# Row sort on one core: the key minimum of the other lot stands between the two masked copies of a lot

## What is computed

```python
q1, k1, q2, k2, v = jnp.split(qkv, 5, axis=1)
vf = v.reshape(b, c, hw)
idx = jnp.argsort(vf, axis=-1)
vs = jnp.take_along_axis(vf, idx, axis=-1)
gat = lambda t: jnp.take_along_axis(t.reshape(b, c, hw), idx, axis=-1)
out1 = _reshape_attn(gat(q1), gat(k1), vs, temperature, True)
out2 = _reshape_attn(gat(q2), gat(k2), vs, temperature, False)
inv = jnp.argsort(idx, axis=-1)
out1 = jnp.take_along_axis(out1, inv, axis=-1)
out2 = jnp.take_along_axis(out2, inv, axis=-1)
```

## Time and profile before

| what | value |
|---|---|
| median of three runs (lowest, highest) | 14898.59 us (14898.33, 14907.5) |
| span of the profiled execution | 14884.8 us |
| DVE busy | 13771.3 us, 93% |
| ACT busy | 7130.0 us, 48% |
| PE busy | 6707.4 us, 45% |
| POOL busy | 6008.9 us, 40% |

### The profile page before, as it was taken

The page is one execution under the profiler, slowest core; times in us unless marked ns, Lnnn a source line. Parts: engine busy times, 40 slices in busy tenths (PEclk is TensorE's granted clock), DMA queues, the critical chain, the costliest instruction groups (busy, mean ns, idle before and its releaser), DMA issues. The chain is left out here.

```text
span 14884.8 us, 121541 instructions
## 1 busy us (share of the span) xinstructions
PE 6707.4 (45%) x42188; PEld 2746.4 (18%) x42188; DVE 13771.3 (93%) x8241; ACT 7130.0 (48%) x6595; POOL 6008.9 (40%) x4372
## 2 busy tenths in 40 slices
PE   4888825750137327426525724814733014433310
PEld 3444401210012112112111212201211002111100
DVE  4888778999999999999999999999999999989978
ACT  0000023455665665565565565565566555444543
POOL 0000000366666666666666666666666630000000
PEclk9999967885568658768757857856966557666655
DMA  2555532100001001001001000100100011221232
GB/s 46 139 144 144 150 78 67 45 27 13 11 12 45 17 12 42 20 12 39 24 12 35 27 12 31 32 12 25 37 12 11 34 33 50 89 66 55 77 76 66
DMA packets 342586, 699.23 MB, mean 47 GB/s; under 512 B 71006, under 2 KB 275007, under 8 KB 331127
## 3 DMA queue, kind: packets, MB, share of 16 engines
q1 hardware_dynamic: 337398, 675.91, 16.8%
q10 hardware_dynamic: 4544, 15.26, 0.4%
HBM read 480.98 MB, written 209.95 MB: 46 GB/s over the span
## 5 line engine op out<-in xcount | busy, mean ns | idle before, releaser
L1191 DVE COPY_PREDICATED arena<-psum,arena 128x4096 f32<-128x4096 uint32 (+26 forms) x1456 | 4010.8, 2772 | 49.1 <-ACT psum L1151 47.8
L1198 DVE COPY_PREDICATED arena<-psum,arena 128x4096 f32<-128x4096 uint32 (+26 forms) x1456 | 3971.8, 2744 | 42.0
L1017 PE MATMUL psum<-arena,wt 128*32 128x448 f32 x31360 | 3213.3, 571 | 1252.6 <-DMA arena<-xpad 699.4
L1116 POOL TENSOR_TENSOR arena<-arena 128x1024 int32<-128x1024 int32 (+26 forms) x1456 | 2079.8, 1435 | 3066.9 <-DVE arena L1183 3065.9
L1102 POOL TENSOR_TENSOR arena<-arena 128x1024 bf16<-128x1024 f32 (+26 forms) x1456 | 1977.4, 1364 | 3029.1 <-SPq L267 2827.4
L1139 ACT ACTIVATE arena<-arena 128x4096 f32<-128x4096 f32 (+26 forms) x1456 | 3071.6, 2126 | 70.1 <-DVE arena L1198 37.4
L1159 ACT ACTIVATE masks<-psum 128x512 fp8e4<-128x512 f32 (+27 forms) x1256 | 924.1, 736 | 3569.2 <-DVE arena L1198 3568.2
L1108 POOL TENSOR_TENSOR arena<-arena 128x1024 int32<-128x1024 int32 (+26 forms) x1456 | 2008.7, 1386 | 0.0
L1017 PEld LDWEIGHTS psum<-arena,wt 128*32 128x32 f32 x31360 | 1043.1, 115 | 3425.3 <-issue 2316.2
L1407 PE MATMUL psum<-ident,arena 128*112 128x128 f32 x896 | 197.1, 385 | 2444.7 <-ACT arena L1326 1882.2
L1183 DVE TENSOR_TENSOR arena<-arena 128x1024 f32<-128x1024 f32 (+26 forms) x1456 | 1166.1, 814 | 99.3 <-POOL arena L1108 99.2
(11 more groups left out here) (132 smaller groups left out, 7666.8 us busy)
## 6 DMA issues: line engine op xcount, KB each, us to landing
arena<-xpad SPq DMA_DIRECT2D x896, 108.5 KB, 2.4
arena<-simd SPq DMA_DIRECT2D x416, 210.0 KB, 4.2
arena<-simd SPq DMA_DIRECT2D x416, 196.0 KB, 4.3
xpad<-arena SPq DMA_DIRECT2D x8, 1924.0 KB, 8.2
arena<-in_x SPq DMA_DIRECT2D x8, 1568.0 KB, 7.8
x3d<-arena SPq DMA_DIRECT2D x8, 1568.0 KB, 5.2
prodd<-arena SPq DMA_DIRECT2D x8, 1568.0 KB, 5.2
arena<-prodd SPq DMA_DIRECT2D x8, 1568.0 KB, 13.5
```

The source lines that it names most:

```text
L1017: last = nc.tensor.matmul(psum[C * b:C * b + C, n % C_BANKS, 0:CROWS * W], wt[:, g, C * w:C * w + C], cx[i % 2][b][:, y0:y0 + CROWS, x0:x0 ...
L1116: last = nc.gpsimd.tensor_tensor(hi, packed_view(stmp, here, piece, 1), lo, ALU.subtract)
L1191: last = nc.vector.copy_predicated(lo, wide_mask(q, k, piece, here), hi)
L1198: last = nc.vector.copy_predicated(hi, wide_mask(q, k, piece, here), packed_view(ptmp, here, piece, NP))
```

## The change

```diff
+            lower_v(0, 0)
             for s in range(SR):
-                lower_v(s, 0)
+                lower(s, 0)
                 next(beside, None)
-                lower(s, 0)
+                lower_v(s, 1)
                 next(beside, None)
                 upper(s, 0)
                 next(beside, None)
-                lower_v(s, 1)
                 lower(s, 1)
                 next(beside, None)
+                if s + 1 < SR:
+                    lower_v(s + 1, 0)
                 upper(s, 1)
                 for _ in range(4, slots):
                     next(beside, None)
```

## The result

The changed kernel takes 14982.03 us (median of 4, 14971.02 to 14988.78), the kernel before 14898.46 us (median of 4 with the new runs, 14892.98 to 14907.5): +83.6 us, a ratio of 1.0056 with a 95% interval of 1.0044 to 1.0068. Slower by clearly more than the 0.2% that can be told. The forecast was 14969 us.

The account below looks back on a forecast made before the run. DVE's row of instructions was taken to bound the kernel. Terms -165 + 123 + 79 + 33 = +70 us on the 14884.8 us span, plus 13.8 to the median, gave 14969 us; range 14846 to 15044.

Parts of the forecast that it names:

- What bounds the kernel: In the row sort, a round is as long as DVE's row of instructions: 1146 of 1176 us.
- Term 1: On DVE, a minimum between lower and upper copy frees the upper copy's start: 0.135 us a lot, -165 us.
- With no gain here: Rival: the upper copy's 0.03 us delay belongs to the copy, not the semaphore; +235 us, 15134 us, chance 0.07.
- Term 2: Moved minima on DVE start while POOL runs and take longer: net 15.5 us a round, +123 us over 8 rounds.
- Term 3: Lower copies wait for ACT's mask words, having less cover: about 10 us a round, +79 us over 8 rounds.
- Term 4: DVE's first multiplication of the other tile comes one lower copy later, delaying PE: 7 x 4.8 = +33 us.
- The sum: All four terms on the whole kernel: +70 us, giving 14969 us, 0.5% slower.
- POOL out of the way: Rival: moved minima meet POOL no oftener than today; -53 us, 14846 us, chance 0.18.
- No change: Rival: half of the costs from POOL meetings and ACT waits; -30 to +30 us, 14869 to 14928, chance 0.24.
- More waiting on ACT: Costs of POOL meetings and ACT waits at upper ends: +145 us, 15044; upper end of the forecast case, chance 0.51.

Follow-up runs that it names:

- Experiment 6: Kernel before, with a one-column memset between the lower and upper copy of each lot, no minimum moved: 14891.23 us, ratio 1.0000.
- experiment 2: Changed kernel, with POOL's sums of lot 0 put behind the upper keys of lot 1 in stages 1 to 65: 14855.95 us, ratio 0.9977.
- experiment 4: Kernel before, DVE's order kept, with POOL's sums of lot 0 put late in stages 1 to 65: 15021.1 us, ratio 1.0090.
- experiment 5: Kernel before, with only lot 1's minimum moved between the copies of lot 0: 15379.03 us, ratio 1.0326.
- Experiment 7: Changed kernel with first slot back, POOL's lot 0 sums late, ACT's mask copy cut to 64 columns (result incomplete): 14741.34 us, against 14824.51 without the cut.
- experiment 1: Changed kernel, with the first slot put back ahead of the lower copy of lot 0: 14932.45 us, ratio 1.0029.

## Why the prediction was right

By its own steps:

- *What bounds the kernel.* Right. The round stayed DVE's row of instructions, and the +82 us of the row sort are found in the spacing and length of what DVE does.
- *Term 1, the hand-over, -165 us.* Right in sign and near in size: about -189, 0.15 us a lot instead of 0.135. The upper copies' idle time went from 42.0 to 0.3 us. Experiment 6 adds a condition that the forecast did not have: an instruction of 0.06 us in between doesn't do. With no gain here the sum would have been 15134 us; the trace showed otherwise before the run, and the run agrees with the trace. The Trainium skill ("VectorE: DVE Perf Modes", The DRAIN you can't avoid) has a measurement in which the semaphore costs nothing extra on this engine, and by it the gain would be nothing. The trace does not agree: the upper copies' idle time of 42.0 us went when the minimum stood ahead of them. The same section adds that a next instruction that is not held starts earlier, and with that the rows agree.
- *Term 2, minima meet POOL, +123.* Measured +145: low by a seventh. The place was right (384 and 408 elements most), and the cause is shown three times, by experiments 2, 4 and 5, in both directions. But the two parts of the term were each off, and that the net came so near is in part luck. The forecast had 26 us a round of new meetings, 208 in all, against 10 a round that go, 80 in all. Minimum by minimum, those that grew by more than 0.05 us grew by 190 us, and those that shrank by as much shrank by only 46. The meeting of the earlier trace rows was to go and stayed: the minimum of stage 2, lot 1, took 2.36 us before, and this is the changed kernel's.

```profile
3958.07 2.35 DVE L1183 TENSOR_TENSOR arena<-arena 128x272 f32<-128x272 f32 x1
```

Of the net +145, 55 us are at 384 and 408 elements and 27 at 448 and 476, where the forecast had 86 and 42. Another 23 are at 512 elements, which it had not named.
- *Term 3, ACT has less time, +79.* Measured +96 as idle time, low by a sixth. Experiment 7 shows that it is ACT's work that decides. The forecast counted on a tie between terms 2 and 3 in one direction only, for its lower end: a delay by POOL gives ACT time. Stage 47 shows the other: 0.7 us of waiting for ACT gave POOL that time.
- *Term 4, +33.* Measured +31 in the profile, and 29 go when it is taken away by itself (experiment 1, whose 43 us hold something else too).
- *The sum, +70.* +83.6 by the medians and +81.8 in the row sort. The errors partly cancelled, and this is luck too: -24 in term 1, -2 in term 4 and -7 in the copies against +22 in term 2, +17 in term 3 and +6 that no term had.
- *Span against median.* The forecast added 13.8 us for what lies around the span. That was no property of the kernel: in the changed kernel's profiled run the time is 14982.58 and the span 14980.7, 1.9 us apart. If the same holds for the kernel before, its profiled execution was a quick one, some 12 us under the median. That fits the 14 us by which its row sort began sooner, at 2770.11 us; in all the other runs it begins at 2776 to 2784.
- *The rivals.* POOL out of the way (14846): its mechanism is real, and experiment 2 brings it about on purpose, at 14856. It failed because in the change as made POOL does meet the minima. No change: the time lies above its 14928. More waiting on ACT: both terms went towards their upper ends, but by +22 and +17 us and not by the +37 and +31 that it had.

One thing was not foreseen: line 1381 (two inputs from the same memory as the minimum) meets POOL too. Its mean is 715 ns in the kernel before, 815 in the changed one, and 1054 in the one of experiment 2, 19 us in all there. In the timeline of the changed kernel it takes 0.68 us where POOL is idle and 0.97 in the mean of the 26 times at which it begins beside POOL. Line 1377, which reads PSUM for one of its two inputs, keeps its 0.69 us in the 49 times at which it begins beside POOL.

## What to carry to other kernels

On this engine an instruction that waits for its neighbour costs about 0.15 us more here (189 us over 1220 pairs) than one that doesn't. A minimum of 0.4 us or more put between the two gets that back, a memset of 0.06 us doesn't. With 1220 such pairs it is worth 1.3% of this kernel. Work that is moved to fill such a gap changes when it meets the engine it shares a path with and how much cover the engines behind the wait have: compare, stage by stage, the time between two of the moved instructions with the length of what the other engine runs between them, and if the second is longer, reorder that engine too. Here the same reordering of POOL was worth -120 us or +129, depending on DVE's order.

## What the runs showed of the hardware that I had not expected

- A minimum on DVE and an instruction on POOL, both with two inputs in SBUF, don't share: the one that starts second waits for the end of the first, less about 0.1 us. 0.05 us decide over 1.15 (experiment 4: 2.34 against 1.19 us). The masked copies, with the mask in PSUM, hardly lengthen: both together 7982.6 us before and 7975.3 after, and in the changed kernel a lower copy of 2048 elements takes 2.43 us (median) where POOL is mostly idle beside it and 2.49 where it is mostly busy.
- A memset of one column between two copies of which the second waits for the first costs nothing at all (1248 of them, ratio 1.0000, 0.9990 to 1.0009).
- POOL's differences now wait for ACT's mask words, which they hardly did before. This is the changed kernel's row of the waits in the row sort (4.2 us in 8 waits before):

```profile
POOL arena L1102 <- ACT psum L1151: 173.7, 99, 3.7
```

It is no wait of DVE's, but it moves POOL's work later, towards the next minimum, and may be part of what term 2 had too little. No run here took it away alone, so that is not shown.
